# A GRU and gated-FFN kernel on one core: the last group's down products moved behind its gate and up products, and three edits in the lone steps

## The reference

```python
gi = x_t @ W_ih + b_ih;  gh = h @ W_hh + b_hh      # 256 -> 768 each
r = sigmoid(i_r + h_r);  z = sigmoid(i_z + h_z)
n = tanh(i_n + r * h_n);  h = (1 - z) * n + z * h  # 32 steps, each after the other
gate, up = split(hs @ ternary(w_gate_up).T)        # 256 -> 2 x 1024
g = silu(gate) * up
out = x + (g * rsqrt(mean(g * g) + eps)) @ ternary(w_proj).T   # 1024 -> 256
```

## Time and profile before

| what | us |
|---|---|
| median of 3 runs (346.06 to 346.06) | 346.06 |
| the profiled execution | 346.3 |
| its span | 344.5 |
| TensorE busy | 339.4 (99%) |
| VectorE busy | 233.6 (68%) |
| ScalarE busy | 222.8 (65%) |
| GpSimd busy | 184.0 (53%) |
| DMA | 18.72 MB, mean 54 GB/s |

### The profile page before, as it was taken

The page is one execution under the profiler, slowest core; times in us unless marked ns, Lnnn a source line. Parts: engine busy times, 40 slices in busy tenths (PEclk is TensorE's granted clock), DMA queues, the critical chain, the costliest instruction groups (busy, mean ns, idle before and its releaser), DMA issues.

```text
span 344.5 us, 5631 instructions
## 1 busy us (share of the span) xinstructions
PE 339.4 (99%) x2059; PEld 295.2 (86%) x2059; DVE 233.6 (68%) x462; ACT 222.8 (65%) x438; POOL 184.0 (53%) x156
## 2 busy tenths in 40 slices
PE   8999999999999999999999999999999999999996
PEld 4889988788988889888888889888888888888895
DVE  7578788899677565755667554875558555664866
ACT  5768888886756757555766656566564655756662
POOL 2315571465825446255454446444472554799694
PEclk9999999999999999999999999999999999999999
DMA  7994000045001000140001000010000100010101
GB/s 240 319 410 192 3 0 2 0 148 220 1 2 62 2 0 0 44 142 2 0 0 63 0 2 0 2 63 0 2 0 2 60 1 2 0 64 1 57 6 61
DMA packets 7891, 18.72 MB, mean 54 GB/s; under 512 B 564, under 2 KB 4788, under 8 KB 7352
## 3 DMA queue, kind: packets, MB, share of 16 engines
q1 hardware_dynamic: 7176, 17.97, 13.9%
q10 hardware_dynamic: 688, 0.39, 0.4%
HBM read 14.17 MB, written 4.19 MB: 53 GB/s over the span
## 4 chain that ended last, share of the span: by engine, by line
PE 94%; DVE 3%; ACT 1%; issue 1%; DVEq 0%
PE ps_ffn L1105 30%; PE ps_out L1143 16%; PE ps_rz L1017 7%; PE ps_rz L1022 7%; PE ps_rz L1018 7%; PE ps_n L1017 3%; PE ps_n L1022 3%; PE ps_n L1018 3%; PE ps_rz L1105 2%; PE ps_ffn L1270 2%; PE ps_t L1098 1%; PE ps_ffn L1017 1%; PE ps_ffn L1022 1%; PE ps_ffn L1018 1%; PE ps_n L1055 1%
## 5 line engine op out<-in xcount | busy, mean ns | idle before, releaser
L354 POOL TENSOR_TENSOR hid_lo<-work,hid_hi 128x512 fp32r<-128x512 f32 x62 | 81.7, 1317 | 103.6 <-ACT hid_hi L452 99.6
L1105 PE MATMUL ps_ffn<-st_hi,wguT 128*128 128x512 f32 x236 | 93.7, 397 | 0.3 <-DVE work L737 0.3
L1105 PE MATMUL ps_ffn<-st_lo,wguT 128*128 128x512 f32 x236 | 92.7, 393 | 0.0
L361 POOL TENSOR_TENSOR sq_sum<-sq_sum,work 128x512 f32<-128x512 f32 x55 | 73.2, 1331 | 1.8 <-ACT work L466 0.6
L737 DVE TENSOR_TENSOR work<-work,ps_ffn 128x512 f32<-128x512 f32 x55 | 37.6, 683 | 31.5 <-ACT work L448 31.5
L452 ACT CAST hid_hi<-work 128x512 fp32r<-128x512 f32 x63 | 38.8, 616 | 23.0 <-DVE work L747 23.0
L1105 PEld LDWEIGHTS ps_ffn<-st_hi,wguT 128*128 128x128 f32 x236 | 44.4, 188 | 8.3 <-DVE work L737 0.9
L1105 PEld LDWEIGHTS ps_ffn<-st_lo,wguT 128*128 128x128 f32 x236 | 44.5, 189 | 7.3
L747 DVE TENSOR_TENSOR work<-work,ps_ffn 128x512 f32<-128x512 f32 x63 | 43.2, 686 | 4.7 <-PE ps_ffn L1105 2.8
L1143 PEld LDWEIGHTS ps_out<-wpT,hid_hi 128*128 128x128 f32 x240 | 35.8, 189 | 3.7
L1143 PE MATMUL ps_out<-wpT,hid_lo 128*128 128x256 f32 x240 | 38.8, 284 | 0.0
(11 more groups left out here) (226 smaller groups left out, 716.0 us busy)
## 6 DMA issues: line engine op xcount, KB each, us to landing
out_dram<-o_st SPq DMA_DIRECT2D x7, 512.0 KB, 2.6
xT_all<-in_x_dram SPq DMA_DIRECT2D x1, 3072.0 KB, 17.6
x_ring<-in_x_dram SPq DMA_DIRECT2D x1, 3072.0 KB, 11.5
x_ring<-in_L_ffn_w_gate_up_dram SPq DMA_DIRECT2D x4, 512.0 KB, 8.9
x_ring<-in_L_ffn_w_proj_dram SPq DMA_DIRECT2D x2, 512.0 KB, 11.6
x_ring<-in_x_dram SPq DMA_DIRECT2D x1, 1024.0 KB, 5.4
work<-in_L_cond_W_ih_dram SPq DMA_DIRECT2D x3, 256.0 KB, 4.4
work<-in_L_cond_W_hh_dram SPq DMA_DIRECT2D x3, 256.0 KB, 4.6
```

Of the source, the lines that this page charges most:

```text
L354: nc.gpsimd.tensor_tensor(hid_lo[:, j % RING], hid[:, j % 2], f32(hid_hi[:, j % RING]), ALU.subtract).then_inc(hid_lo_ok, 1)
L361: nc.gpsimd.tensor_tensor(sq_sum[:], sq_sum[:], hid_sq[:, j % 2], ALU.add).then_inc(sq_added, 1)
L1105: mm = pe.matmul(bank, w, group_state(part, G, k), start=(k == 0 and i == 0), stop=(k == KD - 1 and i == 1))
```

## The change

Four things:

- **Last group.** The down products of group 7 leave their places between the gate and up products and come after `U7`: first the hi parts of all eight tiles, then one set of token squares, then the lo parts, the last four tiles' row by row (`late_down`). To keep all eight tiles until then, `hid`, hi and lo parts get buffers of their own, in tensors that are no longer used (`xT_all`, the GRU weights). The last tile is whole again. GpSimd makes the lo parts of tiles 0 to 3, VectorE those of 4 to 7. Each output row has its own signal and DMA.
- **Seeds.** In lone steps the r and z banks of steps 4 to 8 are filled by a ScalarE copy of the bias instead of a TensorE product. The bias is loaded before units 3 to 5 and summed by GpSimd at t = 3, not at t = 6 and 7.
- **Weights.** GpSimd writes units 0 to 2 as four-byte values itself; ScalarE's three casts go, and its sign activations of units 1 and 2 are made in halves.
- **TensorE's order in lone steps.** One state product of n moves between the halves of r; one input product of n moves ahead of the first transposition.

```diff
@@ PE_END @@
+PE_END = ["G0", "C6", "U0", "G1", "U1", "C7", "G2", "U2", "S", "G3", "U3", "G4", "U4", "G5", "U5", "G6", "U6",
+          "G7", "U7"]
@@ @block.tensor, at the end @@
+            pe.wait_ge(o_ok, NG - 1)
+            pe.wait_ge(gsg_ok, HT * NG - 1)
+            for j in range(HT):
+                late_down(hi_of, j)
+            token_squares(NG - 1)
+            for j in (0, 1, 4, 2):
+                late_down(lo_of, j)
+            for s in range(GS):
+                for j in (5, 3, 6, 7):
+                    mm = late_down(lo_of, j, (s,))
+                mm.then_inc(down, 1)
@@ @block.gpsimd @@
+            G = NG - 1
+            pool.wait_ge(limb_3, G)
+            low_part(G, 0)
+            finish(G - 1)
+            low_part(G, 1)
+            for j in range(1, HT):
+                add_square(G, j)
+                if j in (2, 4):
+                    low_part(G, 1 + j // 2)
+            finish(G)
...
             def signed(u):
-                nc.gpsimd.tensor_tensor(q_signed[:], q_kept[:], q_sign[:, u % 2], ALU.mult).then_inc(q_signed_ok, 1)
+                nc.gpsimd.tensor_tensor(unit_part(u, wguT, wpT), q_kept[:], q_sign[:, u % 2], ALU.mult).then_inc(q_w_ok, 1)
@@ @block.scalar @@
+            hidden_square(G, HT - 1)
+            hidden_hi(G, HT - 1)
...
+                if 1 < t < LEAD - 1:
+                    seed_rz(t + 2)
                 state_hi_early(t)
@@ @block.vector @@
-                if n >= 2:
+                if n >= 2 and not is_late(G):
                     dve.wait_ge(hid_sq_ok, n - 1)
                     dve.wait_ge(hid_lo_ok, n - 1)
...
+                for j in range(3, HT):
                     gated(G, j)
                     hidden(G, j)
+                    if is_late(G) and j == HT - 2:
+                        low_part(G, DVE_LOWS[0])
+            for j in DVE_LOWS[1:]:
+                low_part(NG - 1, j)
+            mean_square(NG - 1)
             rows_out(NG - 1)
@@ input_n_part, state_product @@
-                for x_part, w, k in (((hi, wi_hi, part), (hi, wi_lo, part)) if part < 2
-                                     else ((lo, wi_hi, 0), (lo, wi_hi, 1))):
+                for x_part, w, k in (((hi, wi_hi, 0), (hi, wi_lo, 0), (hi, wi_hi, 1)), ((hi, wi_lo, 1),),
+                                     ((lo, wi_hi, 0), (lo, wi_hi, 1)))[part]:
...
+                        if early(t) and k == 0:
+                            pe.matmul(hid, hi[:, 0, :], wh_hi[:, 0, n_cols], start=False, stop=False,
+                                      skip_group_check=True)
...
-                seed_rz(t + 1)
+                if t < 3:
+                    seed_rz(t + 1)
```

More of the change, by code:

```diff
@@ L208, in up_bank, with is_late, hid_of, hi_of @@
             return product_bank(product(G, j, "up"))
[L210 to L216, removed]
+        late = xT_all[:].rearrange("p k t b -> p (k t b)").rearrange("p (i c) -> p i c", c=512)
+        def is_late(G):
+            return G == NG - 1
+        free = [w[:].rearrange("p k n -> p (k n)").rearrange("p (i c) -> p i c", c=512) for w in (wi_hi, wi_lo, wh_hi, wh_lo)]
+        spare = [w[:, i] for w in free for i in range(3)] + [hid_lo[:, i] for i in range(RING)]
+        def hid_of(G, j):
+            return late[:, j] if is_late(G) else hid[:, j % 2]
+        def hi_of(G, j):
+            return spare[j] if is_late(G) else hid_hi[:, j % RING]
+        def lo_of(G, j):
+            return spare[HT + j] if is_late(G) else hid_lo[:, j % RING]
+        last_out = (ps_out[:, 0, :], ps_out[:, 2, :], ps_n[:, 0:D], gate_bank(NG - 1, HT - 2)[:, 0:D])
+        POOL_LOWS, DVE_LOWS = (0, 1, 2, 3), (4, 5, 6, 7)
+        def low_number(j):
+            return 8 * (NG - 1) + POOL_LOWS.index(j) + 1 if j in POOL_LOWS else DVE_LOWS.index(j) + 1
         def state(parts, t):
@@ L287, in _ @@
                     sp.dma_start(x_ring[:, 0:T - XR, :], x[:, XR:T, :]).then_inc(ld_x, 16)
[L288 to L291, removed]
+            for s in range(GS - 1):
+                sp.wait_ge(o_last, s + 1)
+                sp.dma_start(out[:, T - GS + s, :], o_st[:, s, :]).then_inc(stored, 16)
+            sp.wait_ge(stored, 16 * (NG + 3))
         @block.gpsimd
@@ L651, in _ @@
                 hidden_parts(G, 1)
-                for j in range(3, HT if G < NG - 1 else HT - 2):
+                for j in range(3, HT):
                     silu_part(G, j)
@@ L1180, in token_squares @@
                 mm.then_inc(sq_tok, 1)
-            def last_product(half, kind):
-                cols, gate_to, up_to, _ = last_tile(half)
-                if half == "a":
-                    bank_free(product(NG - 1, HT - 1, kind))
-                elif kind == "up":
-                    pe.wait_ge(gsg_ok, HT * NG - 1)
-                row_tile = HT - 1 if kind == "gate" else 2 * HT - 1
-                for k in range(KD):
-                    w = wguT[:, k, row_tile * P:(row_tile + 1) * P]
-                    for i, part in enumerate((st_hi, st_lo)):
-                        mm = pe.matmul(gate_to if kind == "gate" else up_to, w, group_state(part, NG - 1, k)[:, cols],
-                                       start=(k == 0 and i == 0), stop=(k == KD - 1 and i == 1))
-                mm.then_inc(gate if kind == "gate" else up, 1)
@@ L1201, in down_part @@
                 for s in steps:
-                    mm = pe.matmul(ps_out[:, s, :], part[:, j % RING, s * P:(s + 1) * P], wpT[:, j, :],
-                                   start=False, stop=part is hid_lo and j == HT - 1, skip_group_check=True)
-                return mm
-            def last_high():
-                for first in (0, 2):
-                    down_part(hid_hi, hid_hi_ok, HT - 2, (first, first + 1))
-            def last_rows(s):
-                steps = (s, s + 1)
-                down_part(hid_hi, hid_hi_ok, HT - 1, steps)
-                down_part(hid_lo, hid_lo_ok, HT - 2, steps)
-                down_part(hid_lo, hid_lo_ok, HT - 1, steps).then_inc(down, 1)
```

208 lines of the change are left out of this document (65 added, 143 removed).

## The result

The changed kernel took 350.63 us in the median of four runs (348.67 to 351.76) against 346.06 before: slower by 4.6 us in these medians. The ratio on record is 1.0119, with a 95% interval of 1.0096 to 1.0143, which is 3.3 to 4.9 us. The profiled execution took 351.15 us, with a span of 349.3 where before has 344.5.

The account below looks back on a forecast made before the run. TensorE, busy 99% of the span, was taken to bound the kernel. Lone steps -0.75 and last group +1.7 gave +0.95 us: span 344.5 to 345.4, profiled execution 347.25, median 347.0, range 345.4 to 347.9.

Parts of the forecast that it names:

- the waits of the last group: Last group: TensorE waits for U4's bank until 325.97 and for GpSimd's sum of squares until 338.8.
- the gain in the lone steps: Lone steps, t = 0 to 7: all terms sum to -0.75 us, ends -1.1 and -0.3.
- (a): Lone steps: five bias products of 0.23 us leave TensorE for ScalarE copies, no product waits for a seed; -1.15 us.
- (c): Lone steps: one product of n between r's halves removes a 0.11 us hole on seven steps; -0.70 us.
- 4.87 a step: Lone steps: time between starts of r products forecast as 4.87 us instead of 5.08.
- (b): Lone steps: n's third input product ahead of the left transposition delays the r product 0.12 us, eight times; +0.96 us.
- (d): Lone steps: GpSimd's four-byte weights take 2.2 us, making a low state part late once at t = 3; +0.15 us.
- (e): Lone steps: r and z biases loaded ahead of units 3 to 5 and added at t = 3; costed at nothing.
- Rival C: Lone steps: four-byte form takes 2.6 us, low parts or state copies late, only 0.3 gained; 347.5 us, chance 0.13.
- Last group, +1.7: Last group: last products issue 2.15 us later, one output row fewer behind them saves 0.43; +1.7 us.
- The token squares: Last group: four sets of one-column products of squares, about 0.45 us each, become one set; -1.3 us.
- Rival D: Last group: TensorE stands twice, clock falls to 1.2 GHz, the 4.25 us behind take twice that; 351.2 us, chance 0.03.

Follow-up runs that it names:

- e11: e10 with TensorE waiting for GpSimd's low input part only before the two products that read it; 345.57 us.
- e5: Kernel before with ScalarE seeds, GpSimd four-byte weights and the DMA order, without the moved products of n; 347.72 us.
- e12: Kernel before with all lone-step edits including moved products of n, the later low-input wait and e10's extra one-column instructions; 346.19 us.
- e3: e2 with unread 512-column products filling TensorE's stands, two before the last high group and six before the one-column squares; 348.17 us.
- e4: e2 with the one-column token squares moved behind the low products of tiles 0, 1, 4 and 2; 347.06 us.
- e10: e5 with eight one-column activations on ScalarE and eight one-column fills on VectorE added in idle stretches before 5 us; 346.53 us.
- e13: Kernel before with two one-column fills more on VectorE; 347.58 us.
- e2: Kernel before with only the change's last-group edits, lone steps as before; 349.53 us.
- e14: Changed kernel with the later low-input wait and the one-column squares behind four low product groups; 346.76 us.
- e6: e5 with GpSimd's low input part released one r gate earlier; 347.26 us.

## Why the prediction was wrong

The direction was right, and so were the waits of the last group; the gain in the lone steps had the wrong sign, and the size was far off: +0.95 us forecast and 4.6 measured, 4.8 in the profiled execution with 0.9 of it from a late start. By its steps:

**(a) Seeds, -1.15.** Wrong, and the first of two causes on this side. "The sources are two steps old, so no product waits for a seed" is true, but the question was what the seed covered. It was the cover of GpSimd's low input part, whose end at 28.18 stood in the same profile 0.01 behind the seed's start. e11 shows it: with the wait moved, states 3 to 8 take 0.48 less than before, and with the wait as it was, in e5, 0.05 less.

**(a) to (c) together, 4.87 a step.** Wrong as a sum: I subtracted columns from TensorE's stream and did not ask what the loop allows. The rows were there: 3.91 from r product to state, half of the pair's 0.49, and 0.69 from transposition to r product, 4.85 without the time until the result is seen; e11 has 5.00. Only 0.08 of the 5.08 was to be had, and 4.87 lay under the floor.

**(b) and (c), +0.96 and -0.70.** This is the second cause. On the first two steps, where no seed moves, they cost 0.13 and 0.15 together, as if (b) were right and (c) gave nothing; no run has one without the other. On the steps at the floor they cost nothing and bring nothing (5.01 in e12, 5.00 in e11), so (b) was not due eight times either. The term (c) was mis-sized: from r product to n product the block takes 0.87 before (41.11 to 41.98) and 0.94 with the extra product of 0.12 (42.50 to 43.44), so the hole gave 0.05 and not 0.11, and r's sigmoid comes 0.08 later. **(d)** GpSimd's four-byte form took 2.15 (29.40 to 31.55), the lower bound, with nothing late behind it; the estimate by the Trainium skill (GPSIMD Engine Reference, 3.1) was 2.2, and the trace agrees. The Trainium skill gives this figure for two inputs and says nothing of the output's width; here both widths took 2.15. **(e)** held: 1.42 for both bias additions, no wait.

Together the lone steps gave +0.47 instead of -0.75. Rival C had this side nearest and named other reasons, of which none appears.

**Last group, +1.7.** The waits were right to 0.1 us. With the shift of 1.49 taken off, U4 starts at 325.89 (forecast 325.97), the high products end at 337.1 (337.1), the last square at 338.64 (338.68), and the last DMA issues 0.71 behind the last product (0.75). Two terms failed. The token squares: the 0.45 x4 of the earlier trace rows are the squares of two output rows, recorded twice each, and the one set that replaces them has four rows, x8, and takes 0.92. I put 0.45 for it. The count stood in the row, and it is all that e3 has above the forecast: 20.67 - 18.52 = 2.15 = 1.7 + 0.45.

And the clock, 1.5 us. Rival D had the mechanism and its place, with a price of 4.25 and a chance of 0.03. The price was too high, as the clock was high again from 345.5 on and had fallen only at 342.1, and the chance far too low: in four runs of after, only one has 1.0 throughout. "No such stand is in the trace" was a reason not to know, and I used it as a reason for it not to happen. That D's 351.2 lies near the measured 350.63 is luck: a clock priced 2.7 too high stands against seeds, reorderings and squares that were 1.7 too low, and what a run adds by its start. So 3.6 in place of 1.7 is 1.5 of clock and 0.45 of squares.

**Summed:** -0.75 to +0.47 is 1.2 short, +1.7 to +3.6 is 1.9 short, a start 1.0 late in the profiled execution adds to it and a faster landing takes 0.3 off: 3.8 of the 3.9 us between 347.25 and 351.15.

## What to carry to other kernels

Before work is taken off the busiest engine, look at what becomes ready while it runs: if a result of another engine lands within it, the work was its cover and its time may turn into a wait. In a recurrence, add up the loop from one product to the same product of the next step, and let no forecast go below it. And try two edits of one place together and apart: here the seeds cost nothing alone and the loss came with the reorderings.

Do not let TensorE stand in front of a dense tail if that can be helped: either give it the work whose data are there, as e4 does, or let it compute into a free bank, which was worth 1.4 us here. And put a wait in front of the first instruction that needs it, not of the block; that one move took 0.40 off the lone steps of e10, which was level with before, and made the fastest kernel (e11).

## What the runs showed of the hardware

- Two one-column fills on VectorE at 2 us cost 1.13 us at the end (e13): the last output row lands after 3.1 us instead of 2.0, and a packet of the instruction queue lies in this transfer, as in all five traces with 3.1 and in none of the eleven others. A difference of 1 us in a kernel whose instruction streams agree may be this, and the landing column shows it.
- The granted clock fell to 0.54 behind stands of 0.61 and 1.44 us, and not in every run: 1.0 in one of four runs of after and in one of six of e2. The short stand alone (0.62, e4 and e14) left it at 0.998 or more in 23 runs. The runs of e2 spread over 2.8 us, those of e3, which differs only in the filled stands, over 0.5.
- GpSimd and a VectorE operation with two SBUF operands hold each other up: 1.14 for 0.74 and 1.23 for 0.68 at 31.19 and 31.64 in e6.
